# Relation softmax of a graph network: lanes written out, backward scans into the lane, maxima picked by predicated copies

## What is computed

```python
score = S_src[src, etype] + S_dst[dst, etype] + s_rel[etype]
seg = dst * r + etype
seg_max = jax.ops.segment_max(score, seg, num_segments=n * r)
seg_max = jnp.where(jnp.isfinite(seg_max), seg_max, 0.0)
ex = jnp.exp(score - seg_max[seg])
denom = jax.ops.segment_sum(ex, seg, num_segments=n * r)
alpha = ex / denom[seg]
```

## Time and profile before

| | us |
|---|---|
| median of 3 executions | 8291.74 |
| fastest and slowest of them | 8230.95, 8294.77 |
| the profiled execution, its own time | 8250.71 |
| its span in the profile | 8248.9 |

### The profile page before, as it was taken

One profiled execution on the slowest core, in us unless ns is written; L12 is line 12 of the kernel. 1 busy time (PEld: TensorE's weight loads), 2 busy tenths in 40 slices (PEclk: granted clock), 3 DMA queues, 4 the chain that ended last, 5 costly groups with the idle time before them and its releaser, 6 DMA issues. The chain is left out here.

```text
span 8248.9 us, 101168 instructions
## 1 busy us (share of the span) xinstructions
PE 3484.3 (42%) x20097; PEld 2716.4 (33%) x20099; DVE 3757.1 (46%) x8522; ACT 2123.0 (26%) x5629; POOL 3625.4 (44%) x3965
## 2 busy tenths in 40 slices
PE   3445544545444444444355457324233334333332
PEld 1344444444233334334232223112222223222322
DVE  5444444445644444444664347796233333223333
ACT  1333333333144434334322224255000001000001
POOL 1444443443154444443026650022666664566664
PEclk8676767677756656556666669656555566655556
DMA  3333333333332222222111111001111112111111
GB/s 115 118 104 104 109 108 103 109 107 101 106 92 83 81 84 81 81 80 75 48 51 32 32 36 58 18 0 67 43 44 44 44 45 77 57 44 45 45 44 49
DMA packets 371112, 569.20 MB, mean 69 GB/s; under 512 B 86858, under 2 KB 247772, under 8 KB 370524
## 3 DMA queue, kind: packets, MB, share of 16 engines
q0 software_dynamic: 140272, 311.94, 13.8%
q1 hardware_dynamic: 230764, 256.45, 9.4%
HBM read 509.24 MB, written 58.86 MB: 69 GB/s over the span
## 5 line engine op out<-in xcount | busy, mean ns | idle before, releaser
L682 POOL DMA_INDIRECT ring<-kv_table,idx x1568 | 1494.9, 953 | 1950.7 <-ACT pv L771 1268.1
L2017 POOL DMA_INDIRECT rows_in<-rel_table,idx x1568 | 1489.4, 950 | 808.3 <-issue 610.3
L1196 PE MATMUL ps_s<-rows_in,onehot 128*128 x3520 | 741.0, 393 | 1622.0 <-SPq L2033 850.6
L1196 PEld LDWEIGHTS ps_s<-rows_in,onehot 128*128 128x128 f32 x3520 | 683.0, 296 | 1680.0 <-issue 1679.0
L891 DVE TENSOR_TENSOR key<-ps_q,key 128x528 f32<-128x528 f32 x440 | 306.8, 707 | 1524.2 <-remote 1070.6
L1223 DVE TENSOR_TENSOR acc<-acc,ps_s 128x128 f32 x880 | 253.0, 288 | 1478.8 <-PE ps_s L1196 1065.2
L815 PE MATMUL ps_s<-pv,lent 128*128 128x136 f32 x3520 | 819.4, 386 | 106.6 <-DVE acc L874 94.9
L829 PE MATMUL ps_q<-qsplit,st 128*128 x5280 | 503.7, 255 | 739.9 <-DVE key L891 348.8
L815 PEld LDWEIGHTS ps_s<-pv,lent 128*128 128x128 f32 x3520 | 704.0, 279 | 145.7 <-DVE acc L874 118.1
L829 PEld LDWEIGHTS ps_q<-qsplit,st 128*128 128x128 bf16 x5280 | 413.3, 113 | 826.9 <-issue 801.3
L1726 PE MATMUL ps_f<-s_split,at_lo 128*128 128x392 bf16 x2112 | 510.6, 402 | 357.1 <-DVE found L1783 248.5
(11 more groups left out here) (322 smaller groups left out, 5058.1 us busy)
## 6 DMA issues: line engine op xcount, KB each, us to landing
dl_row<-dloc_slots SPq DMA_DIRECT2D x132, 640.0 KB
eb<-in_edge_attr SPq DMA_DIRECT2D x440, 128.0 KB
ring<-kv_table,idx POOLq DMA_INDIRECT x1568
rows_in<-rel_table,idx POOLq DMA_INDIRECT x1568
flags<-flag_rows SPq DMA_DIRECT2D x88, 168.0 KB
rel_table<-y_out SPq DMA_DIRECT2D x14, 1024.0 KB, 4.3
lo_row<-lo_rows SPq DMA_DIRECT2D x44, 256.0 KB
rel_table<-y_out SPq DMA_DIRECT2D x14, 768.0 KB, 3.6
```

The lines of the kernel that those rows point to most:

```text
L682: pool.indirect_dma_start(ring3[:, s % (2 * RING), :], None, kv_table, bass.IndirectOffsetOnAxis(ap=idx[:, s:s + 1], axis=0))\
L1196: last_mm = pe.matmul(to, one(n, j), ring_rows(places[m], j), start=(j == 0), stop=(j == 1))
L2017: pool.indirect_dma_start(rows3[:, t, :], None, table, bass.IndirectOffsetOnAxis(ap=idx[:, t:t + 1], axis=0))\
```

## The change

The hardware loops of `edge_softmax` are written out: the groups of four lanes stand one after the other in the instruction stream, with constant addresses and constant waits. The distance of lane r is now kept: it goes as a BF16 number (BIG where the type isn't r) to lane r of a new tile `other_t`, and is subtracted from the scores in place of being added with its sign. The backward scan reads `lane_t` and writes the lane of `f_t` directly, without the copy. The pick is a chain: after lane r has its maxima, COPY_PREDICATED overwrites it with lane r - 1 wherever `other_t` of lane r, read as bits, isn't zero. So an edge's own maximum moves on from lane to lane, and the last lane holds it for every edge. `first_t`, `second_t` and `m_t` are gone, `lane_t` (four buffers) takes their place.

```diff
--- before.py
+++ after.py
@@ -989,9 +989,8 @@
                 a_t = sb(done, "a_t", [P, heads * SP])
                 f_t = sb(done, "f_t", [P, lanes * SP])
                 U = 4
-                first_t = [sb(done, "first_t", [P, SP]) for _ in range(U)]
-                second_t = [sb(done, "second_t", [P, SP]) for _ in range(U)]
-                m_t = sb(done, "m_t", [P, SP])
+                lane_t = [sb(done, "lane_t", [P, SP]) for _ in range(U)]
+                other_t = sb(done, "other_t", [P, lanes * SP], BF16)
                 ends = sb(done, "ends", [P, lanes])
                 totals = sb(done, "totals", [P, lanes])
                 ends_r = sb(done, "ends_r", [lanes, P])
@@ -1006,7 +1005,7 @@
                 ready = signal("sm_ready")
                 s3 = score[:, :].rearrange("e (s h) -> e s h", h=heads)
                 a3 = a_t[:, :].rearrange("p (h s) -> p h s", h=heads)
-                lane_of = lambda t, r: t[:, bass.ds(r * SP, SP)]
+                lane_of = lambda t, r: t[:, r * SP:(r + 1) * SP]
                 with nc.Block() as block:
                     @block.tensor
                     def _(pe):
@@ -1048,7 +1047,7 @@
 
 
                             start = count[0]
-                            with dve.Fori(0, lanes // U) as i:
+                            for i in range(lanes // U):
                                 to_do = [body(i * U + u, u) for u in range(U)]
                                 issued = 0
                                 for j in range(per_lane):
@@ -1075,10 +1074,10 @@
                             if not by_relation:
                                 scores = lane_of(a_t, r)
                             else:
-                                far, scores = first_t[u][:, :], second_t[u][:, :]
-                                of = [lambda: dve.tensor_scalar(far, et16_t[:, :], iota_row[:, bass.ds(r, 1)], -BIG,
+                                far, scores = lane_of(other_t, r), lane_t[u][:, :]
+                                of = [lambda: dve.tensor_scalar(far, et16_t[:, :], iota_row[:, r:r + 1], BIG,
                                                                 ALU.not_equal, ALU.mult),
-                                      lambda: dve.tensor_tensor(scores, far, a_t[:, :], ALU.add)]
+                                      lambda: dve.tensor_tensor(scores, a_t[:, :], far, ALU.subtract)]
                             return of + [lambda: dve.tensor_tensor_scan(lane_of(f_t, r), reset_t[:, :], scores, -BIG,
                                                                         ALU.add, ALU.max)]
                         lane_loop(3 if by_relation else 1, forward)
@@ -1108,30 +1107,34 @@
 
                         def backward(r, u):
 
-                            f, whole, back = lane_of(f_t, r), first_t[u], second_t[u]
-                            return [lambda: dve.scalar_tensor_tensor(whole[:, :], cumreset_t[:, :], carry[:, bass.ds(r, 1)], f,
+                            f, whole = lane_of(f_t, r), lane_t[u]
+                            return [lambda: dve.scalar_tensor_tensor(whole[:, :], cumreset_t[:, :], carry[:, r:r + 1], f,
                                                                      ALU.add, ALU.max),
-                                    lambda: dve.tensor_tensor_scan(back[:, ::-1], close_t[:, ::-1], whole[:, ::-1], -BIG,
-                                                                   ALU.add, ALU.max),
-                                    lambda: dve.tensor_scalar(f, back[:, :], 0.0, None, ALU.add)]
-                        lane_loop(3, backward)
+                                    lambda: dve.tensor_tensor_scan(f[:, ::-1], close_t[:, ::-1], whole[:, ::-1], -BIG,
+                                                                   ALU.add, ALU.max)]
+                        lane_loop(2, backward)
                         carries(1, cumclose_t)
 
                         def maxima(r):
                             f = lane_of(f_t, r)
-                            return lambda: dve.scalar_tensor_tensor(f, cumclose_t[:, :], carry[:, bass.ds(r, 1)], f,
+                            return lambda: dve.scalar_tensor_tensor(f, cumclose_t[:, :], carry[:, r:r + 1], f,
                                                                     ALU.add, ALU.max)
                         if by_relation:
-                            link(dve.memset(m_t[:, :], 0.0))
-
-                            def pick(r, u):
-                                own = first_t[u][:, :]
-                                return [maxima(r),
-                                        lambda: dve.scalar_tensor_tensor(own, et16_t[:, :], iota_row[:, bass.ds(r, 1)],
-                                                                         lane_of(f_t, r), ALU.is_equal, ALU.mult),
-                                        lambda: dve.tensor_tensor(m_t[:, :], m_t[:, :], own, ALU.add)]
-                            lane_loop(3, pick, serial=True)
-                            link(dve.tensor_tensor(a_t[:, :], a_t[:, :], m_t[:, :], ALU.subtract))
+                            def last_maximum(r):
+                                to_do = [maxima(r)]
+                                if r:
+                                    to_do.append(lambda: dve.copy_predicated(lane_of(f_t, r), lane_of(other_t, r).bitcast(mybir.dt.uint16), lane_of(f_t, r - 1)))
+                                return to_do
+                            issued = {}
+                            for r in range(lanes):
+                                for step, do in enumerate(last_maximum(r)):
+                                    if r and step:
+                                        dve.wait_ge(chained.sem, chained.at(max(issued[r], issued[r - 1])))
+                                    do().then_inc(chained.sem, 1)
+                                    count[0] += 1
+                                    issued[r] = count[0]
+                            dve.wait_ge(chained.sem, chained.at(count[0]))
+                            link(dve.tensor_tensor(a_t[:, :], a_t[:, :], lane_of(f_t, lanes - 1), ALU.subtract))
                         else:
                             def subtract(r, u):
                                 return [maxima(r),
```

## The result

| | before | changed |
|---|---|---|
| median us | 8282.09 (22 executions) | 8236.55 (22 executions) |
| fastest and slowest | 8230.95, 8312.67 | 8201.36, 8276.58 |
| span of the profiled execution | 8248.9 | 8206.6 |

What follows compares the result with a forecast made beforehand. The uncovered VectorE softmax chain was taken to put its gain straight on the span: 2.0 forward + 10.5 backward + 21.5 pick = 34 us. From 8291.74 us that gives 8257.7, from 8271 8237; 8250 us was taken, range 8195 to 8283.

Steps and rivals of the forecast that it cites:

- What bounds it: Softmax stage: nothing overlaps the VectorE chain, so each microsecond taken from it comes off the span.
- Loop edges: Idle time at the edges of looped lane groups goes when written out: 2.0 us in each pass.
- Direct scan: Backward pass: the scan writes f_t directly, so sixteen copies back fall away, 8.5 us gained.
- BF16 distances: Forward pass: storing and reading distances in BF16 costs nothing and gives nothing, counted as 0.
- the bound of 8 us: Forward pass: loss if the BF16 store fell to a two-operand instruction's rate, 16 x (1.09 - 0.62).
- Pick: Pick pass: maxima alternating with fifteen COPY_PREDICATED, 2.19 us per lane; 55.55 us becomes 34.0, gain 21.5 us.
- c: Price of one predicated copy in the pick chain, taken as 1.09 us; gain = 34 - 15 x (c - 1.09).
- Rivals 1: Pick chain: a predicated copy costs 0.55 us, a one-source copy's rate; gain 42 us; chance 0.06.
- 2 (1.94 us): Pick chain: a predicated copy costs 1.94 us, the scan's rate; gain 21 us; chance 0.10.
- 3 (5.77 us): Pick chain: a predicated copy is microcoded at the reciprocal's rate, 5.77 us; kernel 36 us slower; chance 0.02.
- rival 4: RGCN stages behind: code moved 16 places doubles VectorE's 146.2 us issue idle; kernel 112 us slower; chance 0.02.
- The middle of the four times: Level of the kernel before: middle of the profiled and three timed executions, 8271 us, giving a forecast of 8237.

Runs made afterwards that it cites:

- the sixfold copies: Changed kernel with each predicated copy issued six times in a row, each waiting for the one ahead: stage 236.54 us, whole 1.0077 of the kernel before.
- the pair with GpSimd: Changed kernel with distances on GpSimd and copies one lane behind, 0.9968 of the kernel before, beside the changed kernel, 0.9947; stages 163.1 and 148.6 us.

## Why the prediction was right

Lengths of the three passes, each between the instructions that the prediction named:

| | before | forecast | measured after |
|---|---|---|---|
| forward | 58.76 | 56.8 | 5322.91 - 5266.10 = 56.81 |
| backward | 58.75 | 48.2 | 5374.20 - 5325.94 = 48.26 |
| pick | 55.55 | 34.0 | 5411.77 - 5377.22 = 34.55 |

- **What bounds it.** Nothing runs beside the chain, so a microsecond in it is one of the whole. Shown by the sixfold copies and by the pair with GpSimd, at 0.67% expected against 0.77% (0.53% to 1.01%) and 0.21% against 0.21%, and by the stretch behind the chain, which does not shrink when the chain grows.
- **Loop edges.** Forecast 2.0 us in each of the first two passes and some 6 in all; the written-out loops alone gave 5.62 in the stage, plus the 0.23 ahead of the first distance, which the forward pass in the table includes.
- **Direct scan.** Forecast 8.5, measured 8.51.
- **BF16 distances.** Counted at 0: TENSOR_SCALAR 682 ns against 681, and the subtraction 1084 against 1085. Right, and the bound of 8 us did not enter.
- **Pick.** Forecast 21.5, measured 21.0. The one term off is c, 1.153 us and not 1.09: 15 x 0.063 = 0.9 us, of which the maxima behind a copy, which start 0.11 us before its end and not 0.084, and their shorter mean (1139 ns for 1148) give 0.4 back. Rivals 1 (0.55 us), 2 (1.94 us) and 3 (5.77 us) are all excluded by that one row.
- **Later loops.** 2792.1 and 2793.0 us: no cost from the moved code. The eleven profiles, with different code in this block, have 2792 to 2805 us there, far from the 146 us that rival 4 would add.
- **Sum.** 34 forecast; 33.2 in the stage plus 0.23 in front of it, and 38 (25 to 51) by the ratio. The gain was therefore right for the reason given. The level was not known so well: 8250 us was forecast and 8236.55 measured, 13 us less. Less than 2 us of that come from the level of the kernel before (8250 + 34 = 8284, its median over 22 executions 8282). The other 12 us are the difference of the two medians, 45.5 us where the stage accounts for 33.4, and no run shows a cause for them but scatter. The middle of the four times then known, less 34, would have been 8237; that it lands on the measured median is luck. The prediction also held that a measurement tells only some 1% from no change; with 22 executions each the interval is 0.16% to either side.

The rule of the Trainium skill ("VectorE: DVE Perf Modes", The DRAIN you can't avoid), measured there on eight copies, that waits on the own engine's last instruction are free did not hold: with them gone from fourteen of the fifteen places, the stage was 1.68 us shorter.

## What to carry to other kernels

Where one engine works alone between two block ends, add up its chain from start to start in the timeline and not from busy times: overlap, waits and loop edges are then in the sum, and the forecast here was right to 0.6 us in 34. Before shortening such a chain further, look who is idle beside it and at which price that engine does the same work at this shape: ScalarE took over sixteen instructions for 9.5 us of gain, GpSimd cost 16. Gains of half a percent can be shown by the stage in one execution of each kernel. By whole times one execution tells nothing: 22 of each were compared on the first chip, and five against twelve on the one with the least scatter.

## What the runs showed of the hardware that was not expected

- GpSimd's TENSOR_SCALAR on 128x896 takes 3.3 to 4.6 us against VectorE's 0.68, and slows VectorE's scans while it runs: four in 9.26 us against 7.76. ScalarE at about 1 us slows nothing measurable.
- SCALAR_TENSOR_TENSOR takes 1147 ns at this size with a per-partition scalar from a tile and F32 operands (`carry`), and 1086 ns with a constant and one operand in BF16 (the distances from ScalarE). The two differences were not run apart.
- The kernel before took 8282, 8326, 7979 and 6962 us in four sessions; the changed kernel's softmax stage is equal to a hundredth in the three of them where it was profiled. The difference lies ahead of it: the changed kernel's stage began at 5266 us in the first profile and at 3986 in the fastest, 1280 us earlier, and its spans differ by 1274 us (8206.6 and 6932.3). VectorE's line of products in the attention stage was busy the same, with very different idle time, in the changed kernel on the first chip

```profile
L891 DVE TENSOR_TENSOR key<-ps_q,key 128x528 f32<-128x528 f32 x440 | 306.8, 706 | 1490.6 <-remote 1077.6 <-PE ps_q L829 209.9 <-ACT pv L771 157.0
```

and on the fastest:

```profile
L891 DVE TENSOR_TENSOR key<-ps_q,key 128x528 f32<-128x528 f32 x440 | 305.4, 706 | 545.7 <-PE ps_q L829 293.2 <-ACT pv L771 244.7 <-issue 5.1
```

"remote" has no releaser in the profile. What makes one chip slower there wasn't tried.
